# A delta-rule attention layer with a dense network: taps read from PSUM, state updates summed on TensorE

## The chip, the cores and the metric

The kernel runs on one core of a Trainium2 chip, in float32. The metric is the device time in microseconds (us) of one execution. TensorE, VectorE, ScalarE and GpSimd stand in the profile as PE, DVE, ACT and POOL; PEld is TensorE's loading of weights, and SP issues the DMAs.

## What is computed

The input is x of shape (4, 512, 256). With xn = layernorm(x) the output is x + attention(xn) + ffn(xn). The two parts that matter here are the projections with their short convolution, and the recurrence; there are 16 heads and 4 sequences, so 64 pairs, each with a state S of 128 by 128.

```
q, k, v = silu(causal_conv4(xn @ W.T) + bias)      k scaled by 1/sqrt(128)
a = sigmoid(xn @ Wa.T + ba)      beta = sigmoid(xn @ Wb.T + bb)
for t in 0..511:
    Sk = S k_t
    S  = a_t * S - beta_t * (Sk - v_t) k_t^T       (a_t scales the rows of S)
    o_t = S q_t
```

The outputs o are normalised, gated and projected; the feed-forward part is a gated network with small experts. Neither is touched.

## The kernel before, in words

The program has four stages: layernorm and the dense network; the projections (lines 588 to 632 on ACT, 868 to 878 on DVE, 1180 to 1188 on PE, 480 to 506 on POOL, 348 to 364 on SP); the recurrence; and the output projection. The order of the work on each engine is written out by hand, and semaphores join them. Each engine carries out its own list strictly in order.

**Projections.** Time is cut into 8 pieces of 64 steps. In one piece PE makes 48 jobs for q, k and v (one head each, 4 x 67 columns, with 3 columns of halo) and then 8 jobs for a (two heads each, 4 x 64 columns a head). A job fills one of the 8 PSUM banks in turn; each product of matrices is two MATMUL instructions in float32, and it has two halves in depth, so a job of q, k or v is 4 instructions and a job of a is 8. ACT takes a job of q, k or v with two instructions: a copy of the bank to PRE in SBUF (line 604), and the last tap with the bias into ACC (line 605); then the bank is free (job_free). DVE works on quads of four heads: three rounds of a multiply-add (line 878), ACC += PRE shifted * weight, 12 instructions a quad and 144 a piece. ACT then applies Silu to a whole quad (line 619). After the last quad ACT applies Sigmoid to the 16 heads of a (line 596) straight from PSUM into AST. POOL multiplies k by beta (line 487) as the k quads get ready, and at the end of a piece makes running products of a (lines 490 to 506) into SFST and EST. SP stores the results; ACT may overwrite AST only when the stores of AST and of SFST have landed (lines 629 and 630).

**Recurrence.** Time is cut into 16 chunks of 32 steps, each of 8 blocks of 4 steps (m = 0 to 7). DVE carries the steps of a block (lines 948 to 1018). PE transposes the block's results (corr_transposes, line 1316), ACT copies them (704), PE makes the corrections (1328) and DVE subtracts them (level_sub, 920) before the next block starts. Between the chunks the 64 states are renewed, in 16 slots of four pairs each. A slot goes through: update on PE (line 1303: four products of depth 32, two slots together), subtraction from S on DVE (state_add, line 926), decay on ACT (line 678, four instructions), transposes on PE (1277), a copy on ACT (683), four products with the next keys and queries on PE (reads_of, 1289), and a copy on ACT (692). U_AT, ADD_AT and READ_AT say in which block each step of a slot stands. PE also makes preparations for later blocks between them (prep: lines 1201, 1202, 1209, 1217, 1239), which ACT or DVE take away. Chunk n = 15 has no state work.

## Time and profile before

| | us |
|---|---|
| median of 3 runs (2976.73 to 2979.72) | 2976.94 |
| the profiled execution's own time | 2981.21 |
| its span | 2979.4 |

| engine | busy us | share | instructions |
|---|---|---|---|
| PE | 2244.8 | 75% | 24976 |
| PEld | 1688.4 | 57% | 24976 |
| DVE | 1992.2 | 67% | 4412 |
| ACT | 1375.2 | 46% | 3128 |
| POOL | 818.7 | 27% | 546 |

By stages of the span: the first runs to 272.8 us, the projections to 940.6, a transition to 969.9, the recurrence to 2596.9, the output projection to 2979.4. The busy shares are averages over stages that have different limits, so each stage is read by itself. The profile's chain of work that ended last is made of PE for 47%, of "issue" for 19%, of ACT for 12% and of DVE for 11% of the span. "PEclk" is the granted clock of TensorE: 1.00 is 2.4 GHz and 0.50 is 1.2 GHz.

### The profile page before, as it was taken

The numbers are of one execution on the slowest core, as the hardware profiler recorded it, in microseconds if no ns is written. First come the engines' busy times: TensorE is split into PE (matmuls) and PEld (weight loads), VectorE is DVE, ScalarE is ACT, GpSimd is POOL, SyncE is SP. The second block draws the span as 40 slices with busy tenths as digits, with TensorE's granted clock in tenths as the row PEclk, the third lists the DMA queues.
The fourth block names the chain that finished last, engine by engine and source line by source line (L and its number), as shares of the span: only waits on it lengthen the run. The fifth ranks groups of instructions, "written<-read, shape, count | busy, mean of one in ns | idle before, by whom it ended". The sixth has DMA issues, their size and how long they took to land.

```text
span 2979.4 us, 67827 instructions
## 1 busy us (share of the span) xinstructions
PE 2244.8 (75%) x24976; PEld 1688.4 (57%) x24976; DVE 1992.2 (67%) x4412; ACT 1375.2 (46%) x3128; POOL 818.7 (27%) x546
## 2 busy tenths in 40 slices
PE   5999778777772776777777677767777776299998
PEld 3455566655552666666666666666666665234443
DVE  5223888889882777777777777777777777613234
ACT  2003667766762344444544453445445444044434
POOL 0000777666667121122212122211222121200000
PEclk9999999999996789888978887898889788599999
DMA  5000444445547243334333332433333333311110
GB/s 213 7 14 36 186 166 168 168 182 203 203 173 268 68 140 131 110 102 133 115 113 117 132 108 92 140 131 113 99 133 115 113 116 115 103 74 70 71 56 21
DMA packets 139512, 359.01 MB, mean 120 GB/s; under 512 B 11312, under 2 KB 92968, under 8 KB 126424
## 3 DMA queue, kind: packets, MB, share of 16 engines
q1 hardware_dynamic: 139176, 354.92, 33.5%
q8 instruction: 192, 3.15, 0.4%
q14 instruction: 96, 0.79, 0.1%
q0 software_dynamic: 48, 0.16, 0.0%
HBM read 226.97 MB, written 128.07 MB: 119 GB/s over the span
## 4 chain that ended last, share of the span: by engine, by line
PE 47%; issue 19%; ACT 12%; DVE 11%; POOL 7%; DMA 3%; SPq 0%; DVEq 0%; ACTq 0%; POOLq 0%
PE PS L1289 9%; ACT arena L678 5%; POOL arena L487 4%; PE PS L1395 4%; PE PS L1422 4%; PE PS L1328 3%; PE PS L1277 3%; ACT arena L683 3%; PE PS L1160 3%; PE PS L1201 3%; DMA arena<-beta_d 3%; PE PS L1303 2%; PE PS L1316 2%; PE PS L1249 2%; PE PS L1217 2%
## 5 line engine op out<-in xcount | busy, mean ns | idle before, releaser
L878 DVE SCALAR_TENSOR_TENSOR arena<-arena,SM 128x256 f32<-128x256 f32 x1152 | 542.0, 551 | 93.6 <-ACT arena L605 93.6
L1187 PE MATMUL PS<-arena 128*128 x2048 | 492.6, 398 | 145.3 <-ACT arena L605 131.3
L1187 PEld LDWEIGHTS PS<-arena 128*128 128x128 f32 x2048 | 390.5, 193 | 247.4 <-ACT arena L605 144.3
L487 POOL TENSOR_TENSOR arena<-arena 128x512 f32<-128x512 f32 x64 | 334.6, 5266 | 458.8 <-ACT arena L619 458.8
L524 POOL TENSOR_TENSOR arena<-arena 128x256 f32<-128x256 f32 x128 | 98.6, 771 | 1266.9 <-DVE arena L976 1266.9
L1289 PE MATMUL PS<-arena 128*128 128x128 f32 x1920 | 312.0, 311 | 113.3 <-ACT arena L683 109.5
L1289 PEld LDWEIGHTS PS<-arena 128*128 128x128 f32 x1920 | 262.4, 212 | 156.8 <-ACT arena L683 151.5
L678 ACT ACTIVATE arena<-arena 128x128 f32<-128x128 f32 x960 | 302.1, 396 | 0.0
L920 DVE TENSOR_TENSOR arena<-arena,PS 128x512 f32<-128x512 f32 x192 | 127.5, 685 | 246.5 <-PE PS L1328 246.4
L658 ACT COPY arena<-PS 128x512 f32<-128x512 f32 x154 | 90.3, 586 | 414.8 <-PE PS L1217 196.6
L605 ACT ACTIVATE arena<-PS,SM 128x256 f32<-128x256 f32 x384 | 238.2, 625 | 0.0
L1277 PE MATMUL PS<-ident,arena 128*128 128x128 f32 x960 | 169.1, 304 | 31.0 <-ACT arena L678 30.7
L1303 PE MATMUL PS<-arena 32*128 32x128 f32 x1920 | 162.4, 316 | 30.3 <-DVE arena L926 30.3
L683 ACT COPY arena<-PS 128x512 f32<-128x512 f32 x240 | 140.2, 584 | 92.8 <-PE PS L1277 90.3
L976 DVE TENSOR_TENSOR arena<-arena 128x384 f32<-128x384 f32 (+2 forms) x384 | 175.4, 457 | 11.0
L704 ACT COPY arena<-PS 128x512 f32<-128x512 f32 (+1 forms) x188 | 91.0, 520 | 188.9 <-PE PS L1316 186.5
L692 ACT COPY arena<-PS 128x256 f32<-128x256 f32 x240 | 89.0, 371 | 186.4 <-PE PS L1289 184.1
L1089 DVE TENSOR_TENSOR arena<-PS,arena 128x512 f32<-128x512 f32 x64 | 44.3, 692 | 194.6 <-ACT arena L769 194.5
L961 DVE TENSOR_TENSOR arena<-arena 128x384 f32<-128x384 f32 (+2 forms) x384 | 173.7, 452 | 0.0
L1328 PE MATMUL PS<-arena 32*128 32x64 f32 x3072 | 129.9, 307 | 57.3 <-ACT arena L704 57.3
L604 ACT COPY arena<-PS 128x268 f32<-128x268 f32 x384 | 161.3, 420 | 22.6 <-PE PS L1187 22.3
L970 DVE TENSOR_TENSOR arena<-arena 128x384 f32<-128x384 f32 (+2 forms) x384 | 162.0, 422 | 6.1
(138 smaller groups left out, 3989.0 us busy)
## 6 DMA issues: line engine op xcount, KB each, us to landing
arena<-g_d SPq DMA_DIRECT2D x128, 512.0 KB, 4.2
vas_d<-arena SPq DMA_DIRECT2D x24, 2048.0 KB, 11.4
arena<-vas_d SPq DMA_DIRECT2D x128, 384.0 KB, 3.4
kq_d<-arena SPq DMA_DIRECT2D x8, 4096.0 KB, 11.4
arena<-kq_d SPq DMA_DIRECT2D x16, 2048.0 KB, 9.4
arena<-beta_d SPq DMA_DIRECT2D x8, 2048.0 KB, 9.9
kb_d<-arena SPq DMA_DIRECT2D x8, 2048.0 KB, 6.6
arena<-kb_d SPq DMA_DIRECT2D x16, 1024.0 KB, 6.2
```

What stands on the lines that cost most here:

```text
L487: tt(kb, KQST[:, pp, NB * s:NB * (s + 1), 0, :], kb, ALU.mult).then_inc(kb_step, 1)
L605: nc.scalar.activation(ACC[:, x % 3, h], raw[:, :, HALO:HALO + PT_], ACT.Identity, bias=CB[:, w, h0:h0 + 1], scale=CW[:, w, KC - 1, h0:h0 ...
L678: ins = nc.scalar.mul(S[:, p, :], S[:, p, :], EX[c][:, 6, p:p + 1])
L683: nc.scalar.copy(STR[:, s % 2].rearrange("k g v -> k (g v)"), bank(6)).then_inc(tr_ready, 1)
L878: nc.vector.scalar_tensor_tensor(acc, PRE[:, x % 2, h, :, i:i + PT_], CW[:, w, i, hh:hh + 1], acc, ALU.mult, ALU.add).then_inc(tap_add, 1)
L961: tt(xs, xs, A[:, :, t].unsqueeze(2).unsqueeze(3).to_broadcast([128, NP, 2, 3 - t]), ALU.mult).then_inc(x_dec, 1)
L976: tt(xs, xs, TMP[:, :, 0:6 - 2 * t].rearrange("v p (e t) -> v p e t", e=2), ALU.subtract).then_inc(x_sub, 1)
L1187: ins = mm(bank(g % 8)[:, cols * k:cols * (k + 1)].rearrange("p (b n) -> p b n", b=B), W4[:, WSLOT[kind], kt, DH * (h0 + k):DH * (h0 + k + ...
L1277: ins = nc.tensor.transpose(bank(6)[:, 128 * gi:128 * (gi + 1)], S[:, 4 * (g0 + gi) + j, :], ident[:, :])
L1289: ins = mm(bank(7)[:, 128 * gi:128 * (gi + 1)].rearrange("v (l x) -> v l x", l=NB), STR[:, s % 2, gi, :], KQ[d][:, :, p0:p0 + 2].rearrange ...
L1303: ins = mm(bank(4 + b)[:, 128 * gi:128 * (gi + 1)], PT32[rows, g0 + gi, :], KBT[rows, g0 + gi, :], start=True, stop=True)
L1328: ins = mm(bank(j)[:, 64 * g:64 * (g + 1)], PTL[rows, 128 * g:128 * (g + 1)], GL[L][rows, 64 * (s * G + g):64 * (s * G + g + 1)], start=Tr ...
```

## The change

**Projections.** The copy to PRE is gone. DVE's three taps read the bank in PSUM themselves, so a bank is free only after the third tap. The jobs of q, k and v now turn through 6 banks, and the jobs of a through the other 2. The jobs of a no longer stand behind the last quad: one follows each of the quads 2 to 9 (A_AFTER). ACT takes such a job with Identity and the bias, and one Sigmoid over the whole of AST (2048 elements a partition) stands at the end of a piece. The wait for the stores of AST and SFST stands before the first job of a, behind quad 2.

**Recurrence.** The update of a slot is now a sum in PSUM: the identity times the four states of the slot (one product of 512 columns), then the four products, each added to it. The keys in KBT are negated when they are copied, so that the sum is S minus the update. DVE's state_add is gone; ACT's decay reads the sum from PSUM and writes S. Slots go as one pipeline: updates 0 and 1 stand at the head of block 1, and update s + 2 stands between the transposes and the reading of slot s. READ_AT starts one block earlier.

```diff
-                        nc.scalar.copy(PRE[:, x % 2, h], raw)
-                        nc.scalar.activation(ACC[:, x % 3, h], raw[:, :, HALO:HALO + PT_], ACT.Identity, bias=CB[:, w, h0:h0 + 1],
-                                             scale=CW[:, w, KC - 1, h0:h0 + 1]).then_inc(job_free, 1)
+                    raw = bank(g % QB, B * (HALO + PT_)).rearrange("p (b n) -> p b n", b=B)
+                    nc.scalar.activation(ACC[:, x % 3, h], raw[:, :, HALO:HALO + PT_], ACT.Identity, bias=CB[:, w, hh:hh + 1],
+                                         scale=CW[:, w, KC - 1, hh:hh + 1]).then_inc(job_acc, 1)
+
+                def decay_job(i):
+                    act.wait_ge(a_full, c * (H // 2) + i + 1)
+                    if i == 0:
+                        act.wait_ge(a_stored, c * 16 + 16)
+                        act.wait_ge(sf_stored, c * 16 + 16)
+                    for k in range(2):
+                        h = 2 * i + k
+                        ins = nc.scalar.activation(AST[:, 4 * h:4 * h + 4], bank(QB + i % 2)[:, PC * k:PC * (k + 1)].rearrange("v (b l t) -> v b l t", b=B, t=BL),
+                                                   ACT.Identity, bias=BA[:, h:h + 1])
+                    ins.then_inc(a_free, 1)
...
                     if x > 0:
                         silu(x - 1)
+                    if A_AFTER[x] is not None:
+                        decay_job(A_AFTER[x])
                 silu(NQ - 1)
-                act.wait_ge(a_stored, c * 16 + 16)
-                act.wait_ge(sf_stored, c * 16 + 16)
-                for g in range(A_JOB, NJ):
-                    job(g)
+                act.wait_ge(a_free, c * (H // 2) + 2 + H // 2)
+                nc.scalar.activation(ASTf, ASTf, ACT.Sigmoid).then_inc(a_ready, 1)
...
-                            nc.vector.scalar_tensor_tensor(acc, PRE[:, x % 2, h, :, i:i + PT_], CW[:, w, i, hh:hh + 1], acc, ALU.mult, ALU.add).then_inc(tap_add, 1)
+                            nc.vector.scalar_tensor_tensor(acc, raw[:, :, i:i + PT_], CW[:, w, i, hh:hh + 1], acc,
+                                                           ALU.mult, ALU.add).then_inc(job_free if i == TAPS - 1 else tap_add, 1)
...
-                        ins = nc.scalar.mul(S[:, p, :], S[:, p, :], EX[c][:, 6, p:p + 1])
+                        ins = nc.scalar.mul(S[:, p, :], bank(4 + s % 2)[:, 128 * gi:128 * (gi + 1)], EX[c][:, 6, p:p + 1])
...
-                    for k, s in enumerate(reads):
-                        if k == 0 and len(reads) > 1:
-                            decay(reads[1])
+                    for s in reads:
                         state_copy(s)
-                        if k < 2:
-                            next_evac()
-                        if 0 < k < len(reads) - 1:
-                            decay(reads[k + 1])
+                        if s + 2 < 16:
+                            decay(s + 2)
+                        next_evac()
                         read_copy(s)
...
-                def state_add(s):
-                    j, g0 = slot_pairs(s)
-                    dst = S.rearrange("v (g j) k -> v j g k", j=4)[:, j, g0:g0 + 4]
-                    dve.wait_ge(up_psum, n * 8 + s // 2 + 1)
-                    tt(dst, dst, bank(4 + s % 2).rearrange("v (g k) -> v g k", g=4), ALU.subtract).then_inc(s_updated, 1)
...
-                    for gi in range(4):
-                        for b in range(2):
-                            j, g0 = slot_pairs(2 * u + b)
-                            rows = slice(32 * j, 32 * j + 32)
-                            ins = mm(bank(4 + b)[:, 128 * gi:128 * (gi + 1)], PT32[rows, g0 + gi, :], KBT[rows, g0 + gi, :], start=True, stop=True)
+                    dst = bank(4 + s % 2).rearrange("v (g k) -> v g k", g=4)
+                    mm(dst, ident[:, :], S.rearrange("v (g j) k -> v j g k", j=4)[:, j, g0:g0 + 4], start=True, stop=False)
+                    for gi in range(4):
+                        ins = mm(dst[:, gi], PT32[rows, g0 + gi, :], KBT[rows, g0 + gi, :], start=False, stop=(gi == 3))
                     ins.then_inc(up_psum, 1)
...
-                    for k, s in enumerate(reads):
+                    if m == 1 and nxt:
+                        update(0)
+                        update(1)
+                    for s in reads:
                         state_transposes(s)
+                        if s + 2 < 16:
+                            update(s + 2)
                         if preps:
                             prep(m, *preps.pop(0))
                         reads_of(s)
```

The new constants are these:

```diff
+QB = 6
+A_AFTER = [None, None, 0, 1, 2, 3, 4, 5, 6, 7, None, None]
-READ_AT = [[], [], [0, 1, 2], [3, 4, 5], [6, 7, 8], [9, 10], [11, 12, 13], [14, 15]]
+READ_AT = [[], [0, 1], [2, 3, 4], [5, 6], [7, 8, 9], [10, 11], [12, 13], [14, 15]]
```

## Rows read from the trace of the kernel before

**Rows 1.** Windows of two stages: stretch, length, busy of PE, PEld, DVE, ACT, POOL, PEclk.

```profile
272.80:940.60 667.80, 492.64 (x2048) 390.52 (x2048) 541.98 (x1152) 453.75 (x1008) 467.02 (x145) 0.90 0.47 181
969.90:2596.90 1627.00, 1156.95 (x21072) 1010.16 (x21072) 1244.99 (x2921) 727.18 (x1841) 335.14 (x384) 0.82 0.35 114
```

**Rows 2.** DVE timeline of one piece: start, length, line, count, idle before and releaser.

```profile
452.28 47.60 DVE L878 SCALAR_TENSOR_TENSOR arena<-arena,SM 128x256 f32<-128x256 f32 x120 [0.69 <-ACT arena L605]
511.23 21.65 DVE L878 SCALAR_TENSOR_TENSOR arena<-arena,SM 128x256 f32<-128x256 f32 x24 [11.35 <-ACT arena L605]
```

**Rows 3.** All executions of line 878: durations in ns, min/median/max.

```profile
L878 DVE SCALAR_TENSOR_TENSOR arena<-arena,SM x1152: 471/478/4250, 279.4 to 905.9; 128x256 f32<-128x256 f32 x192
```

**Rows 4.** POOL timeline, the same piece.

```profile
509.55 2.10 POOL L490 TENSOR_TENSOR arena<-arena 128x1024 f32<-128x1024 f32 x1
...
517.91 4.09 POOL L495 TENSOR_TENSOR arena<-arena 128x1024 f32<-128x1024 f32 x1
```

**Rows 5.** ACT timeline, the same piece.

```profile
454.02 0.65 ACT L605 ACTIVATE arena<-PS,SM 128x256 f32<-128x256 f32 x1
454.48 0.47 ACT L604 COPY arena<-PS 128x268 f32<-128x268 f32 x1
...
499.91 1.06 ACT L619 ACTIVATE arena<-arena 128x1024 f32<-128x1024 f32 x1 [3.69 <-DVE arena L878]
500.99 1.28 ACT L596 ACT_TABLE_LOAD   x1
502.28 5.95 ACT L596 ACTIVATE arena<-PS,SM 128x256 f32<-128x256 f32 x16
```

**Rows 6.** PE timeline, the same piece.

```profile
487.60 14.08 PE L1187 MATMUL PS<-arena 128*128 x64 [0.93 <-ACT arena L605]
503.27 14.82 PE L1187 MATMUL PS<-arena 128*128 x64 [1.60 <-ACT arena L596]
```

**Rows 7.** The page's DMA issues: KB each, median us from issue to landing.

```profile
vas_d<-arena SPq DMA_DIRECT2D x24, 2048.0 KB, 11.4
...
kb_d<-arena SPq DMA_DIRECT2D x8, 2048.0 KB, 6.6
```

**Rows 8.** Groups by line and shape: busy us, mean ns, idle before and releaser.

```profile
L926 DVE TENSOR_TENSOR arena<-arena,PS 128x512 f32<-128x512 f32 x240 | 153.2, 679 | 6.4 <-PE PS L1303 6.4
L911 DVE TENSOR_TENSOR arena<-arena,PS 128x256 f32<-128x256 f32 x256 | 91.7, 415 | 91.9 <-PE PS L1249 91.9
L970 DVE TENSOR_TENSOR arena<-arena 128x256 f32<-128x256 f32 x128 | 54.3, 424 | 3.3
```

**Rows 9.** Windows: one chunk, and a stretch in it at the lower clock.

```profile
1175.50:1277.90 102.40, 75.30 (x1363) 65.86 (x1364) 78.70 (x186) 47.59 (x122) 20.93 (x25) 0.83 0.36 118
...
1195.80:1212.00 16.20, 13.47 (x194) 11.76 (x185) 14.95 (x37) 4.10 (x11) 3.46 (x4) 0.50 0.32 92
```

**Rows 10.** PE timeline of that chunk, from a slot's reading to block 4.

```profile
1227.62 1.16 PE L1289 MATMUL PS<-arena 128*128 128x128 f32 x8 [0.68 <-ACT arena L683]
1228.61 1.04 PE L1316 MATMUL PS<-ident,arena 128*128 128x128 f32 x8
...
1232.22 1.11 PE L1303 MATMUL PS<-arena 32*128 32x128 f32 x16
1233.26 0.66 PE L1277 MATMUL PS<-ident,arena 128*128 128x128 f32 x4
1238.52 0.89 PE L1201 MATMUL PS<-arena 128*32 128x192 f32 x8 [4.60 <-DVE arena L920]
```

**Rows 11.** PE timeline, block 5 of the same chunk: a preparation, a slot's reading.

```profile
1251.90 1.10 PE L1239 MATMUL PS<-arena 128*32 128x64 f32 x64
...
1257.00 1.16 PE L1289 MATMUL PS<-arena 128*128 128x128 f32 x8 [1.44 <-ACT arena L683]
```

**Rows 12.** PE timeline of the dense network, matmuls of 512 columns.

```profile
85.01 1.88 PE L1160 MATMUL PS<-arena 128*115 x4
86.72 1.02 PE L1163 MATMUL PS<-arena 72*115 72x512 f32 x2
```

125 lines of the change are left out of this document (57 added, 68 removed).

## The prediction

> **What bounds the kernel now.** I read the windows by stage first [rows 1]: the projections take 667.8 us, the recurrence 1627.0. The change touches these two alone, and each has a limit of its own.
>
> In the projections DVE is the limit. One piece is 0.69 us of waiting, 120 taps in 47.60 us, 11.35 us of waiting for ACT and PE to work through the jobs of a, and 24 taps in 21.65 us [rows 2]: 81.3 us in all. A tap costs 47.60 / 120 = 0.40 us, and the result is there after 0.48 us [rows 3]. So the last 24 should take 9.5 us; they take 12.1 us more, because POOL's products of a run at the same time [rows 4], and one tap then lasts up to 4.25 us [rows 3]. A piece could be 57.2 us of taps.
>
> In the recurrence a chunk takes 102.4 us, with PE busy for 75.3 and DVE for 78.7 [rows 9]. The PE timeline shows who is late: PE goes from a reading straight into the transposes of the corrections (1228.61) [rows 10] and finds DVE's block done, and between a slot's transposes and its reading it waits 0.68 us for ACT's copy. Blocks 2 to 6 are set by this chain of PE and ACT. DVE is late at three places: block 0, the end of block 7, and block 4, where PE stands for 4.60 us [rows 10]. PE is therefore the engine to whose order time is added or taken.
>
> **The projections, step by step.** DVE's taps: the shape is the same, one operand moves to PSUM. A subtraction of the same 256 columns takes 415 ns with an operand in PSUM and 424 from SBUF alone [rows 8], so I keep 0.40 us (bounds: 0.01 less by these two rows, and 0.05 more, what a tap's 478 ns [rows 3] has over such an operation, in case PSUM adds as much again). POOL: a tap with only one operand in SBUF should not fight with POOL; line 926, which reads PSUM, has a mean of 679 ns for 512 columns [rows 8], with no sign of a 4 us case, though POOL works beside it. So the 12.1 us go.
>
> By the Trainium skill's page "VectorE: DVE Perf Modes", section "The TRN2 errata", a DVE instruction has a fixed part of 120 cycles with a PSUM source against 58 from SBUF, at 0.96 GHz. This speaks against the change: 144 taps would cost 9 us more a piece, of which PE's slower pace hides most, so the sum would be some 25 us higher; it belongs to rival (C). Rows 8 do not show the difference.
>
> PE: the last 64 instructions before and after the Sigmoids pace at 0.217 and 0.229 us [rows 6]; a job of four is 0.91 us, a job of a with eight 1.74. A quad with a job of a then keeps PE busy for 4 x 0.91 + 1.74 = 5.4 us, more than DVE's 12 x 0.40 = 4.8: PE becomes the limit for 8 of the 12 quads. In the others the ring of 6 banks is: the third job of a quad waits for the first bank of the quad before. From the first tap of a quad's last head this is 5 taps and a result (2.47), two jobs and their latency (2.1 with the start), ACT's last tap (0.57) and 0.15 of signals: 5.3 us.
>
> ACT: from line 605 to the next instruction 0.46 us; 16 Sigmoids 5.95; Silu with the next start 1.08; a table load 1.28 [rows 5]. At most 0.46 x 4 + 1.08 + 0.74 = 3.7 us a quad: hidden. At the end of a piece it is not hidden: after the last tap come Silu 1.06, table 1.28 and a Sigmoid of twice Silu's length, about 2.0; 4.3 us in which DVE has nothing.
>
> The moved wait is the new stall. Call the end of that Sigmoid 0. The four new last taps are out at 2.0, quads 1 and 2 follow by 5.3 each, and PE, idle for over 6 us at the piece's end, restarts at half clock for some 4 us (2 us late): ACT comes to the first job of a at about 15.7. It must wait for the store of SFST, which follows POOL's 12.5 us [rows 4] and lands 6.6 (as kb_d, alone) to 11.4 us later (as vas_d, in company) [rows 7]: 19.2 to 23.9. I take 19.2, since the store of AST has by then landed. Behind that wait stand ACT's last taps, and behind these DVE. So quad 3 is complete at 19.2 + 2.7 = 21.9, then come 5.3, six times 5.4, 5.3, the remaining taps 3.7 and the end 4.4: a piece of 73.0 us (to 77.7). Against 81.3 that is -8.3, times 8: -66 us, and about -2 for the first piece, which has no stall. Projections: **-68 us** (-90 to -30).
>
> **The recurrence, step by step.** Removed: 240 subtractions, 153.2 us of DVE [rows 8], 10 us a chunk. They stand mostly where DVE then waits for PE, so they are worth only the 2 us that PE waits for them in block 1. Decay from PSUM: ACT has time beside PE now; nothing.
>
> Added on PE: the old update is 16 instructions in 1.04 us for two slots (1232.22 to 1233.26) [rows 10], because they alternate between two groups of rows and start in pairs, 0.11 us apart. The new one is the identity product, 512 columns and two instructions of 0.43 (four in 1.71 us) [rows 12], 0.86; then eight instructions that all use the same 32 rows, so 8 x 0.11 = 0.9; and two changes between the full array and 32 rows, about 0.17 each by the same timeline (eight transposes at 0.11 should take 0.87, the update starts after 0.97; the 16 should take 0.89, the transposes start after 1.04) [rows 10]. Sum 2.1 us a slot, against 0.52: 16 x 2.1 - 8.4 = 25 us of PE a chunk. Bounds for a slot: 1.4 if its products ran in pairs, 2.3 if each change cost twice that.
>
> The Trainium skill's page "TensorEngine Tiling (Array Packing)", section "Key Properties", says that a change of tiling mode drains TensorE and that different tiles work in parallel. The trace agrees with both: the pairs, and the 0.1 to 0.2 us at each change.
>
> Now block by block, from the end of one block's corrections to the next, U = 2.1, transposes 0.45, reading 0.95, preparations 0.45 to 1.44, the chain of corrections 1.4 (levels 4), 2.2 (8) or 3.6 (16), all read as in rows 10 and 11:
> block 1: 4U + 7.0 = 15.4 (before 11.4);
> block 2: 3U + 8.5 = 14.8 (14.7);
> block 3: 2U + 8.4 = 12.6 (12.6);
> block 4: DVE's 6.25 first, one U hidden in it, then 2U + 8.0 = 18.5 (18.1);
> block 5: 2U + 8.3 = 12.5 (9.9);
> block 6: 2U + 7.5 = 11.7 (11.3);
> block 7: DVE's chain, 6.4 (6.9); block 0 unchanged.
> The sum is +7.0 us. The waits of 0.68 between transposes and reading are already inside: an update fills them. PE's wait of 1.44 before the second reading of a block with keys [rows 11] stays.
>
> The clock is inside too: for 16.2 us of the old chunk it is 0.50, though PE is busy for 13.5 [rows 9], work on parts of the array. The identity products fill the whole array there, so I count blocks 1 and 2 at full clock, and 0.5 for a drop in block 4. Without this blocks 1 and 2 would cost 12 us more. Taken: +7.5 a chunk, times 15 (the last has no state work): **+112 us** (+0 to +290).
>
> **Sum.** 2981.2 - 68 + 112 = 3025 for an execution like the profiled one; it stands 4.3 above the median, so **3021 us**.
>
> **Rivals.** (A) PE's added work fits into its gaps. For: PE stands 102.4 - 75.3 = 27 us a chunk, and 25 are added; DVE loses 10. Against: block 0, the correction chains and the readings with keys keep some 20 of the 27. It decides at U = 1.6, where 15 updates on the path give the 7.5 back. Then the recurrence stays and the projections win: 2977 - 68 = 2909. It is the case on the other side. Chance 0.20.
> (B) The clock stays at half in blocks 1 and 2, with twice the updates in them: +19 a chunk, 2977 - 68 + 290 = 3200. For: PE was busy there and was not given the clock. Against: the full array of the identity products. Chance 0.08.
> (C) The projections don't do what is said: taps from PSUM are longer, or POOL still blocks them, or SFST lands late; -20 in place of -68, with the recurrence as forecast: 3069. Chance 0.17.
> (D) The forecast, 0.55, from 2975 to 3065.
>
> **How the numbers follow.** The range cuts 0.1 on each side: half of (A) below 2915, (B) and the edge of (C) above 3110. About 0.2% is what a measurement of this kernel can tell from no change. Faster: (A) and the lowest part of (D), 0.24. Within 0.2%: 0.06. Slower: 0.70.
>
> **What would show it.** Projections: a piece of 73 us, POOL's line 487 at 1.3 us and not 5.3, taps never above 0.6, one idle stretch of 5 us at a piece's end and one before quad 3 that ends with the landing of SFST; PE busy without a gap in quads 4 to 10. If the stall is absent, a piece is 70; if taps from PSUM take over 0.45, DVE sets the pace. Recurrence: a chunk of 110 us, PE busy for about 95, U of 2.1 in the PE timeline, DVE's waits for line 1328 grown by the 10 us that it lost and the 7 of the longer chunk, and PEclk of 1.00 between the first update and block 4. A chunk under 103 would make the forecast wrong, with U well under 2.1 as the first place to look; one over 115 the clock.

## The result and the profile after

The changed kernel takes 3098.4 us (median of 4 runs, 3094.8 to 3103.0) against 2978.3 for the kernel before beside it: a ratio of 1.040, 95% interval 1.038 to 1.042. It is slower by 120 us. The forecast was slower by 43, at 3021.

First the top of the page of the changed kernel, busy time and share of the span by engine, and then two windows, the projections and the recurrence, with the columns of [rows 1]:

```profile
span 3101.3 us, 68348 instructions
...
PE 2548.2 (82%) x25456; PEld 1844.2 (59%) x25456; DVE 1817.2 (59%) x4172; ACT 1318.5 (43%) x2752; POOL 552.7 (18%) x546
```

```profile
272.00:905.00 633.00, 491.31 (x2047) 395.93 (x2045) 468.71 (x1152) 399.08 (x632) 220.60 (x148) 0.91 0.51 200
939.00:2719.00 1780.00, 1451.97 (x21328) 1150.38 (x21320) 1133.55 (x2652) 724.73 (x1840) 327.42 (x382) 0.88 0.31 104
```

The projections' stage is shorter, 633 us for the 667.8 of [rows 1], with POOL at 221 us of work where it had 467. The recurrence is longer, 1780 for 1627, and in it PE's busy time rose by 295 us while DVE's fell by 111. PE went from 75% of the span to 82%.

Where the 121.9 us between the two profiled executions arise can be counted along one mark, the step of DVE's line 1015 in each block. Its first execution comes 47.5 us earlier than before (936.7 against 984.2 us). From there to the last block of the last chunk the recurrence takes 169.9 us more. The output stage is the same to 0.5 us. So the change is the sum of two halves of opposite sign: **-47.5 for the projections, +170 for the recurrence**; the forecast had -68 and +112.

**The projections.** The stage by groups of instructions (count, then busy us and mean ns, then idle time ahead and what ended it):

```profile
L886 DVE SCALAR_TENSOR_TENSOR arena<-PS,SM,arena 128x256 f32<-128x256 f32 x1152 | 468.7, 477 | 125.2 <-ACT arena L594 122.4
L485 POOL TENSOR_TENSOR arena<-arena 128x512 f32<-128x512 f32 x64 | 80.3, 1275 | 496.0 <-ACT arena L619 496.0
L604 ACT ACTIVATE arena<-PS,SM 128x256 f32<-128x256 f32 x128 | 53.9, 475 | 43.0 <-DMA vas_d<-arena 31.9 <-PE PS L1176 11.1
L632 ACT ACTIVATE arena<-arena 128x4096 f32<-128x4096 f32 x8 | 28.9, 3617 | 0.1
```

A tap from PSUM has a mean of 477 ns, against a median of 478 and a worst case of 4250 in [rows 3]; the long cases are gone: the longest tap is 487 ns. POOL's product (line 485, line 487 before) takes 1.275 us for 5.27 before. The third row is the moved wait: ACT's evacuation of a job of a now stands 31.9 us for the landing of a store. The fourth is the one Sigmoid that replaced sixteen, 3.62 us long. It covers 4096 elements a partition; where the section on the change gives 2048, that is my error, and it went into the forecast.

The DVE timeline of one piece (start, length, line, count, idle before):

```profile
495.37 5.77 DVE L886 SCALAR_TENSOR_TENSOR arena<-PS,SM,arena 128x256 f32<-128x256 f32 x14 [6.51 <-ACT arena L594]
502.03 0.48 DVE L886 SCALAR_TENSOR_TENSOR arena<-PS,SM,arena 128x256 f32<-128x256 f32 x1 [0.89 <-ACT arena L594]
503.56 4.80 DVE L886 SCALAR_TENSOR_TENSOR arena<-PS,SM,arena 128x256 f32<-128x256 f32 x12 [1.05 <-ACT arena L594]
508.78 3.62 DVE L886 SCALAR_TENSOR_TENSOR arena<-PS,SM,arena 128x256 f32<-128x256 f32 x9 [0.42 <-ACT arena L594]
515.74 5.77 DVE L886 SCALAR_TENSOR_TENSOR arena<-PS,SM,arena 128x256 f32<-128x256 f32 x14 [3.34 <-ACT arena L594]
...
529.35 4.94 DVE L886 SCALAR_TENSOR_TENSOR arena<-PS,SM,arena 128x256 f32<-128x256 f32 x12 [0.43 <-ACT arena L594]
```

Against [rows 2], the 24 taps in 21.65 us are no more. In their place stand 6.51 us at the end of a piece (Silu 1.05, table load 1.28, Sigmoid 3.62, first tap 0.57), 3.34 us ahead of quad 3 for the store, and 0.42 us a quad, 5.37 from quad to quad where a job of a goes with it. The pieces start 74.5 to 76.2 us apart, 75.4 in the mean (81.3 before), but the first takes 70.5 where it had taken 69.3.

**The recurrence.** Three windows: a usual chunk, one of the two long ones, and in the latter the time at the lower clock. A chunk is counted here from the mark (line 1015) of block 7 to that of the next block 7. The two long ones have block 1 at the lower clock. Columns as in [rows 9]; the granted clock is the number after the last count, 1.00 for 2.4 GHz and 0.50 for 1.2:

```profile
1379.10:1491.70 112.60, 94.28 (x1403) 74.72 (x1401) 71.71 (x169) 47.97 (x122) 20.44 (x24) 0.91 0.33 107
1145.70:1266.50 120.80, 102.21 (x1400) 80.14 (x1400) 71.70 (x169) 47.63 (x121) 20.41 (x24) 0.83 0.30 100
1154.50:1181.80 27.30, 22.03 (x254) 15.99 (x254) 15.38 (x44) 6.39 (x17) 4.36 (x6) 0.50 0.37 126
```

Twelve chunks take 111.3 to 113.5 us, two 120.8 and 122.7, the last is as before; [rows 9] has 102.4. PE's busy time is up by 19 us, DVE's down by 7. And one slot on PE, then the start of block 4 and the end of block 6, in PE's timeline:

```profile
1440.90 1.02 PE L1303 MATMUL PS<-arena,ident 128*128 128x512 f32 x2
1441.86 1.15 PE L1305 MATMUL PS<-arena 32*128 32x128 f32 x8
1446.52 0.89 PE L1201 MATMUL PS<-arena 128*32 128x192 f32 x8 [3.51 <-DVE arena L929]
...
1478.21 1.02 PE L1303 MATMUL PS<-arena,ident 128*128 128x512 f32 x2
1479.16 1.15 PE L1305 MATMUL PS<-arena 32*128 32x128 f32 x8
1480.25 0.66 PE L1209 MATMUL PS<-ident,arena 128*128 128x128 f32 x4
1482.35 2.08 PE L1290 MATMUL PS<-arena 128*128 128x128 f32 x8 [1.44 <-ACT arena L686]
```

From the identity product's start to the next instruction is 1480.25 - 1478.21 = 2.04 us a slot, where the old update had two slots in 1.04 [rows 10]. No idle time stands ahead of either: PE does these one after the other. Two waits do stand here, 3.51 us for DVE and 1.44 for ACT. Both were there before [rows 10, 11], and now PE works at the lower clock behind both. The granted clock up to the middle of the first wait, from there on, and behind the second:

```profile
1436.00:1444.50 8.50, 6.28 (x94) 5.03 (x93) 6.44 (x11) 3.55 (x10) 0.46 (x1) 1.00 0.23 64
1444.60:1451.40 6.80, 4.88 (x69) 4.61 (x70) 6.66 (x14) 0.96 (x2) 2.70 (x3) 0.50 0.02 5
1482.10:1488.90 6.80, 6.09 (x37) 5.21 (x38) 2.23 (x6) 2.97 (x9) 0.52 (x1) 0.50 0.47 154
```

The reading of 8 instructions at 1482.35 takes 2.08 us where the same takes 1.16 at the full clock.

Only the lower clock at the second place is new. The kernel before had 6.8 us of it at the first place too:

```profile
1236.00:1243.00 7.00, 4.48 (x68) 4.21 (x68) 6.86 (x17) 0.96 (x2) 2.64 (x3) 0.51 0.01 4
```

The preparation of 0.89 us in [rows 10] ran in it; the same takes 0.56 at the full clock (e6 below). At the second place the kernel before kept the full clock: it has 30 waits of 1.44 us, and behind none of them is the clock lower; its lower stretch at the end of a chunk (3.4 us, from 1273.7) began 7 us behind such a wait. The changed kernel has 30 of them as well, two a chunk, and the clock is 0.50 behind 13 of the 15 that stand second in their chunk, and behind none of the 15 that stand first.

### The profile page after: what moved, and what is told of

It reads as the page before. It is cut to its first block, busy times and chain, and to the rows that moved or that the text cites. A ratio compares the mean times of both kernels' runs of the same rounds, so it can differ in the third digit from the quotient of the medians.

```text
span 3101.3 us, 68348 instructions
## 1 busy us (share of the span) xinstructions
PE 2548.2 (82%) x25456; PEld 1844.2 (59%) x25456; DVE 1817.2 (59%) x4172; ACT 1318.5 (43%) x2752; POOL 552.7 (18%) x546
## 4 chain that ended last, share of the span: by engine, by line
PE 60%; issue 17%; DVE 8%; POOL 6%; ACT 5%; DMA 3%; SPq 0%; DVEq 0%; POOLq 0%; ACTq 0%
PE PS L1305 8%; PE PS L1290 8%; PE PS L1303 7%; PE PS L1330 4%; PE PS L1278 4%; PE PS L1395 3%; PE PS L1422 3%; PE PS L1239 3%; PE PS L1153 3%; POOL arena L485 2%; PE PS L1201 2%; PE PS L1318 2%; DMA arena<-beta_d 2%; PE PS L1249 2%; PE PS L1217 2%
## 5 line engine op out<-in xcount | busy, mean ns | idle before, releaser
L886 DVE SCALAR_TENSOR_TENSOR arena<-PS,SM,arena 128x256 f32<-128x256 f32 x1152 | 468.7, 477 | 125.2 <-ACT arena L594 122.4
L1176 PEld LDWEIGHTS PS<-arena 128*128 128x128 f32 x2048 | 396.5, 195 | 193.7 <-DVE arena L886 113.4
L681 ACT ACTIVATE arena<-PS,arena 128x128 f32<-128x128 f32 x960 | 275.4, 373 | 278.1 <-PE PS L1305 277.3
L929 DVE TENSOR_TENSOR arena<-arena,PS 128x512 f32<-128x512 f32 x192 | 127.5, 685 | 422.2 <-PE PS L1330 422.0
L1305 PEld LDWEIGHTS PS<-arena 32*128 32x128 f32 x1920 | 236.0, 189 | 186.5 <-issue 186.5
L1290 PEld LDWEIGHTS PS<-arena 128*128 128x128 f32 x1920 | 263.9, 213 | 76.0 <-ACT arena L686 57.0
L1305 PE MATMUL PS<-arena 32*128 32x128 f32 x1920 | 282.3, 287 | 0.0
L594 ACT ACTIVATE arena<-PS,SM 128x256 f32<-128x256 f32 x384 | 208.1, 567 | 152.7 <-PE PS L1176 149.1
L1303 PE MATMUL PS<-arena,ident 128*128 128x512 f32 x480 | 255.7, 615 | 0.0
L686 ACT COPY arena<-PS 128x512 f32<-128x512 f32 x240 | 141.1, 588 | 113.8 <-PE PS L1278 109.1
L661 ACT COPY arena<-PS 128x512 f32<-128x512 f32 x94 | 55.1, 586 | 295.6 <-PE PS L1217 201.6
L1330 PE MATMUL PS<-arena 32*128 32x64 f32 x3072 | 122.9, 297 | 65.8 <-ACT arena L707 65.8
L485 POOL TENSOR_TENSOR arena<-arena 128x512 f32<-128x512 f32 x64 | 80.3, 1275 | 496.0 <-ACT arena L619 496.0
L1330 PEld LDWEIGHTS PS<-arena 32*128 32x128 f32 x3072 | 106.7, 204 | 97.0 <-ACT arena L707 88.6
## 6 DMA issues: line engine op xcount, KB each, us to landing
kq_d<-arena SPq DMA_DIRECT2D x8, 4096.0 KB, 11.4
```

The source lines that it names most:

```text
L594: nc.scalar.activation(ACC[:, x % 3, h], raw[:, :, HALO:HALO + PT_], ACT.Identity, bias=CB[:, w, hh:hh + 1], scale=CW[:, w, KC - 1, hh:hh ...
L681: ins = nc.scalar.mul(S[:, p, :], bank(4 + s % 2)[:, 128 * gi:128 * (gi + 1)], EX[c][:, 6, p:p + 1])
L886: nc.vector.scalar_tensor_tensor(acc, raw[:, :, i:i + PT_], CW[:, w, i, hh:hh + 1], acc, ALU.mult, ALU.add).then_inc(job_free if i == TAPS ...
L1176: ins = mm(dst.rearrange("p (b n) -> p b n", b=B), W4[:, w, kt, DH * h:DH * (h + 1)], XNT[:, kt, :, bass.ds(c * PT_ + (HALO - halo), halo ...
L1290: ins = mm(bank(7)[:, 128 * gi:128 * (gi + 1)].rearrange("v (l x) -> v l x", l=NB), STR[:, s % 2, gi, :], KQ[d][:, :, p0:p0 + 2].rearrange ...
L1303: mm(dst, ident[:, :], S.rearrange("v (g j) k -> v j g k", j=4)[:, j, g0:g0 + 4], start=True, stop=False)
```

## The experiments

Each kernel was timed against the kernel before on its chip (2979 to 2981 us). "A chunk" is the time between the marks named above. A *stretch* goes from one mark to the next and bears the number of the block whose mark ends it; stretch 0 runs from block 7's mark to the next block 0's. The prediction and the table further down count a *block* from one block's corrections to the next, which is mostly the stretch with a number one higher: block 4 is mostly stretch 5. The expected texts use both, under the name of block. What three of them call beta passes are the jobs of a.

**The halves apart.** e1 has the projections' half and the old recurrence:

```diff
-NJ = len(JOBS)
+NJ = 4 * NQ
+QB = 6
+A_AFTER = [None, None, 0, 1, 2, 3, 4, 5, 6, 7, None, None]
-        nc.vector.scalar_tensor_tensor(acc, PRE[:, x % 2, h, :, i:i + PT_], CW[...], acc, ALU.mult, ALU.add)
+        raw = bank(g % QB, B * (HALO + PT_)).rearrange("p (b n) -> p b n", b=B)
+        nc.vector.scalar_tensor_tensor(acc, raw[:, :, i:i + PT_], CW[...], acc, ALU.mult, ALU.add)
```

> The kernel before with the projections' half of the change alone (the taps read the projection's accumulator in PSUM, ACT makes the first tap from it; the recurrence is as before). My theory, from the two traces: a piece goes from 81.3 us to about 75.5 in seven of the eight (the first had never been held up, 69 to 70 us), and the transition gives a few us more, so -47 to -50 us: about 2930. The forecast's step said -68: 2910. Rival: the halves act on each other (the later start of the recurrence moves the clock), then the projections alone give less than 40 us, over 2938. A POOL operation of the line that replaced 487 has 1.3 us and not 5.3, and no tap is over 0.6 us.

Measured: 2929.9 us, a ratio of 0.983 (0.982 to 0.985): -51 us. POOL's product has 1.28 us, the taps 0.48, the pieces are 74.5 to 76.2 us apart. This half is a gain, and to the first mark of the recurrence it is the whole kernel's, 48 us for 47.5; the rest of the 51 comes behind the mark.

e2 has the recurrence's half and the old projections:

```diff
-                for gi in range(4):
-                    for b in range(2):
-                        ins = mm(bank(4 + b)[...], PT32[rows, g0 + gi, :], KBT[rows, g0 + gi, :], start=True, stop=True)
+                mm(dst, ident[:, :], S.rearrange(...)[:, j, g0:g0 + 4], start=True, stop=False)
+                for gi in range(4):
+                    ins = mm(dst[:, gi], PT32[rows, g0 + gi, :], KBT[rows, g0 + gi, :], start=False, stop=(gi == 3))
```

> The kernel before with the recurrence's half of the change alone (state updates summed by TensorE with the identity, decay by ACT from PSUM, one pipeline; the projections are as before). My theory, from the two traces: 15 chunks of 112.6 in place of 102.4 (+153) and two of them at half clock in block 1 (+8 each), so +165 to +172 us: about 3147. The forecast's step said +112: 3090. A time between 3090 and 3120 would say that the change's halves are worse together than apart. DVE's wait for the accumulation's product line is then near 28 us a chunk, from 16.

Measured: 3148.0 us (3136.9 to 3152.7), a ratio of 1.057: +167. DVE's wait for the correction product was 383.9 us over 1600 us, 27 a chunk. In the profiled execution no chunk was a long one, all took 111.5 to 113.1, and the recurrence is 153 us longer, 15 times 10.2. It is also the fastest of the four, at a granted clock of 0.909; the others stand 10 to 16 us higher at 0.902 to 0.904, which is the size of one or two long chunks, but there is no trace of them. The halves add up, -51 + 167 = 116 against 120 for the whole, so no action of one on the other is seen beyond some 4 us, and what is left to explain is mostly in the recurrence.

**What the taps' place does.** e8 is e1 with a copy to SBUF in between:

```diff
+        nc.scalar.copy(PRE[:, x % 2, h], raw)
         nc.scalar.activation(ACC[:, x % 3, h], raw[:, :, HALO:HALO + PT_], ACT.Identity, ...)
-        raw = bank(g % QB, B * (HALO + PT_)).rearrange("p (b n) -> p b n", b=B)
+        raw = PRE[:, x % 2, h]
```

> The projections' half of the change alone, but ACT copies each projection to SBUF first and the taps read that copy (one added ACT copy a job, 0.7 us; the first tap by ACT and POOL's work stay). It tells what the taps' place does. Theory: DVE's taps with both operands in SBUF and POOL's adds hold one another up, as in the kernel before: single taps up to 4 us, POOL's operation back at 4 to 5 us, and a piece back at 80 us or above: 2970 to 2990. Rival: the gain came from the fewer operations of DVE and ACT, not from where the taps read: within 15 us of 2930.

Measured: 3087.1 us (one run), 157 more than e1; the direction was as expected, the size three times that. A piece takes 95.4 to 96.4 us. One row of DVE's timeline and three of POOL's beside it:

```profile
547.33 18.30 DVE L888 SCALAR_TENSOR_TENSOR arena<-arena,SM 128x256 f32<-128x256 f32 x14 [6.79 <-ACT arena L598]
```

```profile
550.85 4.10 POOL L494 TENSOR_TENSOR arena<-arena 128x1024 f32<-128x1024 f32 x1
555.02 4.08 POOL L496 TENSOR_TENSOR arena<-arena 128x1024 f32<-128x1024 f32 x1
559.19 2.48 POOL L500 TENSOR_TENSOR arena<-arena 128x256 f32<-128x256 f32 x2
```

The same 14 taps take 5.77 us from PSUM, beside the same operations of POOL. The 12.5 us between the two is DVE held up beside POOL: taps of 2.23, 4.24, 4.24 and twice 1.36 us run beside POOL operations of 2.19, 4.10, 4.08, 1.20 and 1.32. Four later quads of the piece have 2.0 us more each beside POOL's products; together that is the 20 us by which a piece is longer than in e1. POOL hardly suffers: its product has 1.43 us on average, where it had 5.27 in the kernel before; why the kernel before had the other pattern, POOL slow and only the taps at a piece's end held up, stays open. So the projections' gain comes from the operand in PSUM; and DVE's own pace says that this operand costs nothing. The Trainium skill's page "SBUF — State Buffer", section "Who interferes with whom", has the rule: the two engines share a pair of ports, and a DVE instruction with at most one input in SBUF, outside the two-port modes, doesn't contend for it. The two timings of the 14 taps agree with that.

**The moved wait.** e7 is e1 with the jobs of a two quads later:

```diff
-A_AFTER = [None, None, 0, 1, 2, 3, 4, 5, 6, 7, None, None]
+A_AFTER = [None, None, None, None, 0, 1, 2, 3, 4, 5, 6, 7]
```

> The projections' half of the change alone, with the eight passes that put the beta of the last piece (a-jobs) two quads later (beside quads 4 to 11 and not 2 to 9), so that ACT has no wait for the stored tile at quad 2. Theory: the 3.3 us that DVE stands still ahead of quad 3 in each of seven pieces go: -3 to -4 a piece, about 2905 to 2909 against 2930 with the projections' half as it is. Rival: the passes then lie beside the last quads and delay the piece's end, or the ring's slots bound these quads in any case: 2925 or above.

Measured: 2905.5 us, a ratio of 0.975 (0.973 to 0.976). The idle time ahead of quad 3 is gone and all pieces but the first are 71.8 us apart, 3.6 less than the 75.4 of e1. The stall was real, it was PE's and DVE's path, and two quads of distance remove it.

**The price of a slot's update.** e3 leaves the identity product out, and with it the old state's part of the sum:

```diff
-                    mm(dst, ident[:, :], S.rearrange("v (g j) k -> v j g k", j=4)[:, j, g0:g0 + 4], start=True, stop=False)
-                        ins = mm(dst[:, gi], PT32[...], KBT[...], start=False, stop=(gi == 3))
+                        ins = mm(dst[:, gi], PT32[...], KBT[...], start=True, stop=True)
```

> The changed kernel without the product of the identity with the old state in each slot's update (left out: the old state in the sum; the four products of a slot start their own sums; everything else, decay and copies too, stays). If the update is bound by PE's own instructions, 16 identity products of about 0.95 us and 16 changes between the full array and 32 rows of 0.1 to 0.17 us go: -16.8 us a chunk to 96, and about 2850 in all. Rival, the clock: without the full-array products PE's clock drops to half in blocks 1 and 2 as it did in the kernel before, and 5 to 9 us a chunk come back: 101 to 105 a chunk, 2920 to 2985. Rival, ACT or DVE bound the update: under 5 us a chunk go, above 3020.

Measured: 2934.3 us (one run), 164 below the changed kernel. Two neighbouring chunks:

```profile
1022.90:1123.80 100.90, 81.95 (x1372) 72.22 (x1372) 71.75 (x169) 48.27 (x123) 22.44 (x24) 0.86 0.36 119
1123.80:1227.80 104.00, 85.45 (x1369) 75.07 (x1367) 71.78 (x170) 47.40 (x122) 22.42 (x24) 0.82 0.35 116
```

8.6 to 11.7 us a chunk go, not 16.8: time and chunk are those of the second case, the clock's. PE's busy time falls by 12.3 us in the better chunk, and the granted clock from 0.91 to 0.86 and 0.82. The first updates run at half clock, as they did before the change. How much of the missing 5 to 8 us the clock takes was not isolated.

e4 issues the updates of two slots together, the products alternating between their row groups:

```diff
-                    mm(dst, ident[:, :], S...[:, j, g0:g0 + 4], start=True, stop=False)
-                    for gi in range(4):
-                        ins = mm(dst[:, gi], PT32[rows, ...], KBT[rows, ...], start=False, stop=(gi == 3))
+                    for b in range(2):
+                        j, g0 = slot_pairs(s + b)
+                        mm(dst[b], ident[:, :], S...[:, j, g0:g0 + 4], start=True, stop=False)
+                    for gi in range(4):
+                        for b in range(2):
+                            j, g0 = slot_pairs(s + b)
+                            rows = slice(32 * j, 32 * j + 32)
+                            ins = mm(dst[b][:, gi], PT32[rows, ...], KBT[rows, ...], start=False, stop=(gi == 3))
```

ACT's decays stand one slot later to go with it.

> The changed kernel with the updates of two slots issued together: two identity products one after the other (into the two banks), then the eight pairs' products alternating between the two slots, which lie in different 32-row groups. If products of one row group wait for one another and those of two groups don't, eight products take about 0.45 us in place of 0.9, and half of the changes between the array's shapes go (0.17 each): U for two slots from 4.2 to about 3.1 us, -8 to -9 us a chunk, -120 to -135 in all: about 2970. Rival: products of a slot are bound by something other than the row group (issue, the writes to one bank): only the mode changes go, -2.7 a chunk, about 3058. Rival: the pair of updates waits for ACT's copies of two slots, and what PE saves is lost in waits: 3090 or above.

Measured: 3047.7 us (3045.7 to 3051.2): -51 against the changed kernel, not -125. The pair of updates on PE, and the next instruction:

```profile
1161.94 1.88 PE L1301 MATMUL PS<-arena,ident 128*128 128x512 f32 x4
1163.76 1.16 PE L1306 MATMUL PS<-arena 32*128 32x128 f32 x16
1164.85 0.65 PE L1237 MATMUL PS<-arena 128*32 128x64 f32 x32
```

Two slots take 2.91 us, where two of 2.04 are 4.08: sixteen instructions over two row groups take what eight over one do. The row group sets the pace, as supposed, and as the Trainium skill has it on its page "TensorEngine Tiling (Array Packing)", section "Key Properties": different tiles work in parallel. The products of one row group start 0.11 us apart in both kernels. Eight pairs are 9.4 us a chunk. The best chunk of this execution has 106.3 us for 112.6, so 6.3 of the 9.4; ahead of the first slot's transposes PE now waits 1.2 us for ACT. But only some chunks are like it:

```profile
1136.00:1242.30 106.30, 84.79 (x1403) 67.00 (x1404) 71.72 (x169) 47.09 (x123) 22.37 (x24) 0.92 0.33 113
1242.30:1356.60 114.30, 93.34 (x1401) 73.64 (x1399) 71.78 (x170) 46.64 (x122) 22.36 (x24) 0.82 0.32 105
```

The same 1400 instructions keep PE busy for 84.8 us in one chunk and 93.3 in the next, and the granted clock is 0.92 and 0.82, while DVE's, ACT's and POOL's busy times agree to 0.5 us. The mean of the execution's chunks is 110.2 us, so 3.9 of the 6.3 us are lost in the chunks with the lower clock. Even the best chunk, at 0.92, is 3.9 us longer than the 102.4 of the kernel before.

**The waits and the clock behind them.** e5 moves ACT's copy of a preparation behind the read copy of its slot, which is what PE's wait of 1.44 us is for:

```diff
                     for k, s in enumerate(reads):
                         ...
-                        next_evac()
                         read_copy(s)
+                        if evacs and evacs[0][1] == k:
+                            next_evac()
```

> The changed kernel, but ACT copies a preparation's result after the read product of its own slot and not before. In the trace of the changed kernel PE waits 1.44 us for ACT's read copies at two places a chunk (blocks 5 and 6), because the preparation's copy stands ahead of them. My theory: these waits end PE's path there, so -2.9 to -4.2 us a chunk: -45 to -60, about 3045. Rival: PE is then late at its next wait (for the corrections' copies) by as much less, or loses clock in exchange: 3080 to 3100.

Measured: 3055.5 us (3039.8 to 3058.2), -43; just short of the 45 expected, a usual chunk of 109.2 for 112.6 (two take 119.4 and 119.5). Stretches 6 and 7, 12.9 and 12.7 us, are 11.6 and 9.9, and stretch 5 is 18.3 for 18.9. Of the 4.1 us in the first two, the two waits are 2.9, and the rest is PE's clock, which no longer falls at the end of block 6: the reading there takes 1.06 us and not 2.08. Stretch 0 gives 1.6 us back: it takes 15.6 us for 14.0, at a clock that now falls there.

e6 fills the wait at the start of block 4 with products that nobody reads:

```diff
+                        if m == 4 and s == reads[0]:
+                            pe.wait_ge(x_read, n * 16 + s)
+                            for _ in range(13):
+                                mm(bank(7)[:, 0:128], ident[:, :], ones[:, :], start=True, stop=True)
```

> The changed kernel with 13 products of 128 columns, of the identity with a block of ones, into an unused half of the reading bank, put into PE's wait of 3.5 us at the start of block 4 (added work whose result nobody reads, about 2.8 us). In the trace of the changed kernel the clock falls to half 6.8 us long right behind that wait. Theory: the fall comes from the wait; with PE busy in it the clock holds, block 4 takes 18.5 us and not 20.3, and no slot waits: -1.8 a chunk, -27, about 3071. Rival: the fall comes from the partial-array products before and after it (or elsewhere), then nothing goes, or +0 to +1 a chunk come for products that PE hadn't time for: 3098 to 3113.

Measured: 3072.9 us, but from 3060.5 to 3099.4. Block 4 takes 18.4 to 18.5 us in every chunk, the very size expected, where it had taken 20.3 (in stretches, number 5 takes 17.0 for 18.9), so the theory holds for the place. The start of the block:

```profile
1434.22 3.17 PE L1371 MATMUL PS<-ones,ident 128*128 128x128 f32 x26
1437.79 0.56 PE L1201 MATMUL PS<-arena 128*32 128x192 f32 x8 [0.41 <-DVE arena L929]
```

In nine of fourteen chunks the clock then falls in stretch 6 (14.3 to 14.9 us for 12.9), which gives 1.4 to 2.0 back, as the rival said; in the others a chunk is 109.2 to 109.5. Both were right, each in a part of the chunks. The four executions go with the clock: 0.921, 0.920, 0.914 and 0.909 from the fastest to the slowest.

e12 has e5's and e6's edits, and three such products ahead of block 0's corrections:

```diff
+                    if m == 0:
+                        for _ in range(3):
+                            mm(bank(3)[:, 0:128], ident[:, :], ones[:, :], start=True, stop=True)
```

> The changed kernel with the preparations' copies later (e5) and with added products that keep PE busy in two waits of a chunk: 3 ahead of block 0's corrections and 13 in the wait at the start of block 4 (e6). Theory: what the recurrence costs above the forecast is the clock behind PE's waits. With block 4 at 17.0 (e6) and blocks 6 and 7 at 11.6 and 9.9 (e5) a chunk is 107 us, below the 109.9 of the forecast, and the chunks with block 1 at half clock no longer occur or occur less: 3005 to 3025. Rival: the clock falls elsewhere for what it is held here, as behind block 5 in e6: 109 or above, 3040 or above.

Measured: 3012.2 us (3005.9 to 3014.6), a ratio of 1.011 (1.009 to 1.012). Block 4's start, and two chunks:

```profile
1414.44 3.17 PE L1372 MATMUL PS<-ones,ident 128*128 128x128 f32 x26
1418.02 0.56 PE L1202 MATMUL PS<-arena 128*32 128x192 f32 x8 [0.42 <-DVE arena L930]
```

```profile
1350.60:1457.20 106.60, 93.50 (x1428) 75.26 (x1429) 71.83 (x169) 47.00 (x122) 20.46 (x24) 0.95 0.36 119
1457.20:1565.40 108.20, 94.30 (x1438) 75.58 (x1437) 71.78 (x169) 47.38 (x123) 20.45 (x24) 0.95 0.33 107
```

The same preparation after the wait is 0.56 us long, and was 0.89. All chunks take 106.5 to 108.9 us, no long one among them, in the mean 107.6, 5.0 less than the changed kernel's usual one, and 2.9 of these are the waits that e5 took away. With the clock held, a chunk with the waits would by this be near 110.5, an estimate; the forecast had 109.9.

**The same helps in the old recurrence.** e9 is e7 with ACT's copies moved as in e5:

```diff
-                        if k < 2:
-                            next_evac()
                         ...
                         read_copy(s)
+                        if k < 2:
+                            next_evac()
```

> The kernel before's recurrence, the projections' half of the change with its beta passes two quads later (as e7), and in the recurrence ACT copies a preparation's result after the read product of its own slot. The kernel before has the same two waits of 1.44 us a chunk for ACT's read copies, and eight more of 0.68. Theory: as in the changed recurrence (e5, -3.4 a chunk), 3 to 4 us a chunk go: 2845 to 2865 against 2905. Rival: in the old recurrence DVE's work closes the blocks and PE's waits are not the path: under 1 us a chunk, above 2890.

Measured: 2913.6 us (2909.3 to 2917.7), 8 more than e7. The waits are gone, and a chunk still takes 102.2 to 102.6 us (the last but one 107.1, for 102.9 in e7) at a clock of 0.83 to 0.87: stretch 6 is 12.5 in every other chunk for 10.4, and in the chunks between stretch 0 is 16.4 for 14.3. The theory fell. The rival had the time right and the reason wrong: as e10 shows next, it is PE's clock that holds the chunk.

e10 is e9 with the added products, 3 ahead of block 0's corrections, 16 at block 4, and 6 here:

```diff
                     if m == 1 and nxt:
+                        for _ in range(6):
+                            mm(bank(7)[:, 0:128], ident[:, :], ones[:, :], start=True, stop=True)
                         update(1)
```

> e9 with added products of 128 columns (the identity with ones, read by nobody) in three of PE's waits of a chunk: 3 ahead of block 0's corrections, 6 ahead of block 1's second update and 16 in the wait of 4.6 us at the start of block 4. Theory: the clock's halves at 20 to 37 us and at 61 to 68 us of a chunk come from the waits before them; with the clock held, block 4's products give back 2 us as in e6 and blocks 1 and 2 another 2 to 4: 2780 to 2830, and the granted clock above 0.93. Rival: the clock falls again a little later (as in e6 behind block 5), and the products that don't fit their waits cost what is won: within 15 us of e9, or above it.

Measured: **2859.9 us** (2855.8 to 2868.4), a ratio of 0.960 (0.958 to 0.963). Below the range expected for the gain, 54 us and not 80 or more, and the clock 0.917. One chunk of it, and then 22 us of it from stretch 1 to stretch 3, and the same 22 us of the kernel before:

```profile
1391.90:1490.30 98.40, 75.24 (x1421) 66.38 (x1419) 78.56 (x185) 47.64 (x122) 20.84 (x24) 0.91 0.37 122
```

```profile
1408.00:1430.00 22.00, 18.80 (x384) 16.50 (x379) 19.94 (x48) 7.05 (x17) 5.52 (x8) 0.79 0.24 74
```

```profile
1396.00:1418.00 22.00, 18.43 (x326) 15.99 (x322) 19.66 (x46) 6.97 (x16) 5.35 (x6) 0.60 0.27 74
```

PE does 58 instructions more in the same time, 18 of them added products and the others work that came later before, and is busy for hardly longer, at a clock of 0.79 for 0.60. e10 is the fastest of all kernels here, and it needs nothing of the changed recurrence.

e14 is e10 without e9's edit.

> e10 without the later copies of the preparations (so e7 with the added products alone: 3 ahead of block 0's corrections, 6 ahead of block 1's second update, 16 at block 4). Theory: in the old recurrence these copies don't matter (e9 against e7: +8), so all of e10's gain is the clock's: 2850 to 2865. Rival: the two edits act together, and without the later copies PE's clock falls behind the waits of 1.44 us: 2875 to 2890.

Measured: 2876.9 us (2874.8 to 2879.0), -29 against e7. The time is that of the second case: the later copies, worth nothing alone, are worth 17 us beside the added products. Its reason is not: all 28 waits of 1.44 us that the fourteen chunks have here are followed by the full clock. Stretches 5, 6 and 7 are 0.7, 0.3 and 0.3 us longer than in e10, others vary from chunk to chunk in both; where the 17 us arise was not isolated.

**The changed recurrence at its best.** e11 joins the edits of e4, e5 and e7.

> The changed kernel with three of the edits tried alone: two slots' updates together (e4: -51), the preparations' copies later (e5: -43) and the beta passes two quads later (e7: -24). If they add up, 2980; that would be the kernel before's time, so that the changed recurrence, thus mended, still costs 75 more than the old one with the same projections (e7: 2906). Rival: what PE no longer does is taken back by its clock (already in e4: 6 us a chunk at full clock, 3.6 in the mean), then 3000 to 3030.

Measured: 2969.0 us (ten runs, 2959.0 to 2981.8), a ratio of 0.997 (0.995 to 0.999): the edits add up, and 11 us more. e13 adds e12's products to it (ten at block 4).

> The best version of the changed recurrence (e11) with the same added products, 3 ahead of block 0's corrections and 10 at block 4. Theory: e11 loses 2 to 3 us a chunk to the half clock in block 1, up to 22 us of a chunk: with it held, blocks 1 and 4 give back 2 to 4 us: 2915 to 2940. It then stands beside the old recurrence with the same helps (e10: 2860), and the difference is what the changed recurrence costs: 55 to 80 us. Rival: the clock stays at half from 8.7 to 22.4 us of a chunk, since the wait of 6.7 us in block 0 can't be filled: 2955 to 2970.

Measured: 2961.7 us, 7 below e11, which is not clear of noise (0.993 to 0.996 against 0.995 to 0.999 of the kernel before). Stretch 2 is 1.4 to 2.9 us shorter, as the theory had it, but the time comes back elsewhere: in stretch 7 (11.5 for 9.9) in nine of fourteen chunks, in stretch 3 (14.6 for 13.4) in seven, and in stretch 0 (15.6 for 14.0) in most of the others. The theory's mechanism was seen and its sum was not. The old recurrence with the like helps stands at 2860, so the changed one, with its updates paired, costs 100 us; this is the fairest price of the idea that the runs give.

## Why the prediction was right in its sign and wrong in its size

The steps, in the prediction's order.

**Projections, forecast -68, measured -47 to -51** (profile, e1). Right: a tap from PSUM at a pace of 0.40 us; POOL no longer in DVE's way, shown by e8; POOL's product at 1.3; a quad with a job of a at 5.4 (5.37); the others at 5.3 (5.22); the stall at the moved wait, shown by e7. The fixed 120 cycles for a PSUM source of the Trainium skill's page "VectorE: DVE Perf Modes", section "The TRN2 errata", had been weighed at 9 us a piece; taps with 477 ns from PSUM and 479 from SBUF (e8, median) show none of it here. **The term that was mis-sized is the Sigmoid**: 3.62 us and not 2.0, since I took half of its elements. Eight times 1.6 is 13 of the 20 us that are missing. A piece then is 74.6 by the forecast's own working and 75.4 in the mean, which is 6 more. The count of pieces was wrong too, and luck made it harmless. I multiplied by eight, but the first piece of the kernel before takes only 69.3 us and the new one 70.5. The gain of 5.9 us a piece came six times (35 us); at the two ends it is 12, as much as two pieces more: the first tap comes 5.3 us earlier, the first piece loses 1.3, the last gains 1.8, and the way from the last tap to the first mark of the recurrence is 6.1 shorter. I had read one piece in the middle and neither end.

**Recurrence, forecast +112, measured +167 to +170** (profile, e2). The block model, us a chunk, from the end of one block's products of the corrections (line 1328, 1330 after) to the next; block 7 ends where its transposes begin. Measured are the usual chunks:

| block | before | forecast | measured |
|---|---|---|---|
| 1 | 11.5 | 15.4 | 15.2 |
| 2 | 14.7 | 14.8 | 14.9 |
| 3 | 12.7 | 12.6 | 12.3 |
| 4 | 18.1 | 18.5, and 0.5 for the clock | 20.3 |
| 5 | 9.9 | 12.5 | 12.5 |
| 6 | 11.4 | 11.7 | 13.2 |
| 7 | 6.6 | 6.4 | 6.4 |
| 0 | 17.6 | unchanged | 17.8 |

U was taken as 2.1 and is 2.04. That DVE's relief is worth nothing beyond block 1 fits: its wait for the correction product grew from 246.5 to 422.2 us, 12 a chunk (I had said 17). Blocks 1, 2, 3, 5 and 7 are within 0.3. **The step that failed is the clock's**: "0.5 for a drop in block 4". The drop costs 1.8 us there, 1.3 more than I had put down, since block 4 takes 20.3 as it stands and 18.45 when products fill the wait (e6, e12); and 1.5 came at the end of block 6, where I had none: e5, which takes the wait away, has 10.4 us there, and that is 11.85 with the wait of 1.44 added back. In two chunks of the profiled execution block 1 also ran at half clock, 8 us each. A usual chunk is 10.2 us longer and not 7.5: 15 x 2.7 + 16 = 57 us, which is the difference between 112 and 169. e12, where the clock is held at 0.95, has chunks of 107.6 us, and 110.5 with the waits added back, for the forecast's 109.9.

The reading behind this step was short. I had named one stretch at the lower clock in the old chunk, the 16.2 us of [rows 9]; there were three more, 6.8 us in block 0, 6.8 behind the wait of 4.60 us in block 4, and 3.4 at the end. The block sums were made of terms at the full clock, so the price of the stretch in block 4, which stood in that trace, was missing from 18.5, and 0.5 was not enough for it. The price of a wait on PE is its idle time and what the clock does behind it. The second place could not be read there: behind the old kernel's waits of 1.44 us the clock stayed at 1.00. The Trainium skill's page "TensorE: Matmul & The Clock Gate", section "HAM oscillation — how this bites in real kernels", tells of the same kind of loss, waits (there for DMA) after which the work begins at the lower clock every time. The row at 1444.60 agrees with it. The waits of 1.44 us fit only in part, since behind one of the two in a chunk the clock stays at 1.00.

**The rivals.** (A), the added work fits PE's gaps, needed U below 1.6. e4 brought U to 1.46 a slot, and the kernel then came to 3048, not to 2909: the granted clock was lower than in the changed kernel (0.895 for 0.906), and even the best chunk is 3.9 us above 102.4. So the deciding point was wrong as well; only with e5's and e7's edits too (e11) is the changed kernel level with the one before. (B), blocks 1 and 2 at half clock, was given 0.08 for all chunks; it is what happened in two of fifteen, at the price given (+18.4 and +20.3 us, forecast +19). (C) failed in its causes, but a quarter or more of the forecast's gain in the projections was missing for another reason, the Sigmoid above all. That the time lay inside the range is luck: between 3065, where (D) ends, and 3110 stood only (C), whose causes were not these.

**What stays open.** Why two chunks of fifteen run block 1 at half clock. In both the lower clock lasts 27.3 us instead of 6.8. It begins in the wait of 6.7 us for DVE in block 0, as in the usual chunk at 10.9 us of the chunk: at 8.7 in one of the two and at 10.7 in the other, so an earlier start is not the whole reason. Among the profiled executions it happened in the changed kernel (2 chunks), e5 (2) and e6 (1), and not in e2 or e12; e2's slower executions have no trace. I took every bank of PSUM to hold results in that wait which DVE is still to read, so it wasn't tried to fill it. Open too is why the clock falls behind the second wait of 1.44 us in a chunk and not behind the first.

## What to carry to other kernels

Before work moves from an engine with slack to TensorE, price it there as this trace does, by row group: here one product after another in one group of 32 rows is 0.11 us an instruction, while two groups side by side took the same time for twice the work, and a change to and from the full array came on top. A wait of TensorE that is hidden today can have a second price, the clock behind it; look at the granted clock in the stretch after each wait, in the kernel before as well, and before mending the order of work try products that nobody reads in the wait (here 29 us for three places, and 54 where ACT's copies had been moved too). Where a DVE operation stands beside GpSimd work, an operand that is in PSUM anyway is worth reading there (157 us here); and what a stage repeats should be read in its first, a middle and its last repetition before a gain is multiplied, since the ends can fall out either way.

## What the runs showed of the hardware that I had not expected

- DVE with both tensor operands in SBUF beside GpSimd's operation on SBUF: 14 taps in 18.30 us, and 5.77 with one operand in PSUM, at the same GpSimd operations of 4.1 us. With the operand in PSUM neither is seen to slow the other.
- A kernel with less work on PE can be granted less clock: 0.91 with the identity products, 0.86 and 0.82 a chunk without them (e3); 0.92 and 0.82 in neighbouring chunks of e4 with the same instructions, 106.3 and 114.3 us.
- Added products were paid back at once: 25 products a chunk in three waits of the old recurrence raised the granted clock from 0.83 to 0.91 and shortened the chunk from 102.3 to between 98.4 and 101.0 us (e10 against e9).
- The same wait of 1.44 us for ACT is followed by the lower clock at one place of the changed chunk (13 of 15) and never at the other, 12.5 us earlier, nor at any of the 30 of the kernel before.
- An edit that takes 2.9 us of waits a chunk away can be worth nothing (e9, +8 us in all) and 17 us beside the added products (e10 against e14).
- The same kernel's executions differ by up to 39 us (e6, 3060 to 3099, at granted clocks from 0.921 down to 0.909), while those of the kernel before stay within 8.
